# A perceiver block on one core: a key-first head with half loads, and the last tile's sums split between engines

## The reference

```python
q = (layernorm(x) @ Wq + bq)           # per head
k, v = ctx @ Wk + bk, ctx @ Wv + bv
scores = einsum('bqhd,bkhd->hbqk', q, k) / sqrt(32)
attn = softmax(scores.reshape(16 * 4, 128, 2048), axis=0)
x = x + einsum('hbqk,bkhd->bqhd', attn, v) @ Wo + bo
```

## Time and profile before

| | before |
|---|---|
| time, median of 3 runs (lowest to highest) | 725.75 us (724.75 to 725.82) |
| the profiled execution: time, span | 725.73 us, 723.9 us |
| PE busy | 707.0 us (98%) |
| DVE busy | 627.9 us (87%) |
| POOL busy | 502.2 us (69%) |
| ACT busy | 489.7 us (68%) |
| DMA | 55.74 MB, mean 77 GB/s |

### The profile page before, as it was taken

The page is one execution under the profiler, slowest core; times in us unless marked ns, Lnnn a source line. Parts: engine busy times, 40 slices in busy tenths (PEclk is TensorE's granted clock), DMA queues, the critical chain, the costliest instruction groups (busy, mean ns, idle before and its releaser), DMA issues.

```text
span 723.9 us, 17414 instructions
## 1 busy us (share of the span) xinstructions
PE 707.0 (98%) x7587; PEld 570.3 (79%) x7587; DVE 627.9 (87%) x511; ACT 489.7 (68%) x696; POOL 502.2 (69%) x284
## 2 busy tenths in 40 slices
PE   9999999999999999999999999999999999899987
PEld 8777788888888888888888888887677667778876
DVE  6479999999999999999999999999977467977785
ACT  5578677686776867777686776868543446735682
POOL 0165979999999999999999999995993020054400
PEclk9999999999999999999999999999999999999999
DMA  8310110101101010110101101010002799621101
GB/s 333 129 60 8 53 59 2 60 1 60 43 17 60 2 59 1 60 60 1 60 2 59 41 20 60 2 59 2 2 9 110 278 391 382 252 104 59 59 2 59
DMA packets 15387, 55.74 MB, mean 77 GB/s; under 512 B 1616, under 2 KB 2128, under 8 KB 11728
## 3 DMA queue, kind: packets, MB, share of 16 engines
q1 hardware_dynamic: 15312, 54.64, 20.7%
HBM read 43.16 MB, written 11.47 MB: 75 GB/s over the span
## 4 chain that ended last, share of the span: by engine, by line
PE 79%; DVE 7%; DMA 5%; ACT 4%; POOL 3%; issue 1%; SPq 0%; POOLq 0%; DVEq 0%; ACTq 0%
PE ps L464 24%; PE ps L392 23%; PE ps L497 9%; PE ps L523 8%; DMA rel_scratch<-blocks 5%; POOL s_buf L1307 2%; PE ps L437 2%; PE ps L799 2%; PE ps L373 2%; PE ps L533 1%; PE ps L781 1%; PE ps L381 1%; PE ps L547 1%; DVE extra L1482 1%; PE ps L406 1%
## 5 line engine op out<-in xcount | busy, mean ns | idle before, releaser
L1307 POOL TENSOR_TENSOR s_buf<-s_buf,r_all 128x1024 f32<-128x1024 f32 x93 | 197.2, 2158 | 0.8 <-DVE r_all L1495 0.8
L989 ACT COPY s_buf<-ps 128x1024 f32<-128x1024 f32 x128 | 123.1, 1016 | 27.6 <-PE ps L497 27.6
L1005 ACT ACTIVATE s_buf<-s_buf 128x1024 f32<-128x1024 f32 x128 | 134.3, 1064 | 11.1 <-DVE s_buf L1475 8.0
L1453 DVE TENSOR_REDUCE extra<-s_buf 128x128 f32<-128x2048 f32 x48 | 109.3, 2278 | 4.6 <-ACT s_buf L989 4.6
L1475 DVE TENSOR_TENSOR s_buf<-s_buf,ps 128x2048 f32<-128x2048 f32 x48 | 106.9, 2283 | 0.5
L1274 POOL TENSOR_TENSOR v_buf<-v_buf,extra 128x512 f32<-128x512 f32 x64 | 81.0, 1300 | 6.6 <-ACT v_buf L981 6.6
L1482 DVE TENSOR_REDUCE ps<-s_buf 128x128 f32<-128x4096 f32 x16 | 70.8, 4428 | 14.4 <-ACT s_buf L1005 14.4
L981 ACT COPY v_buf<-ps 128x512 f32<-128x512 f32 x64 | 37.6, 587 | 66.2 <-PE ps L392 65.6
L1285 POOL TENSOR_TENSOR w_lo<-raw,w_hi 128x2048 fp32r<-128x2048 f32 x5 | 23.1, 4621 | 83.5 <-ACT w_hi L956 83.5
L497 PEld LDWEIGHTS ps<-q_t,k_t 32*128 32x128 f32 x2048 | 63.0, 186 | 18.9 <-issue 18.9
L497 PE MATMUL ps<-q_t,k_t 32*128 32x128 f32 x2048 | 75.1, 283 | 0.4 <-ACT k_t L971 0.2
(11 more groups left out here) (244 smaller groups left out, 1469.8 us busy)
## 6 DMA issues: line engine op xcount, KB each, us to landing
rel_scratch<-blocks SPq DMA_DIRECT2D x16, 636.0 KB, 10.9
s_buf<-rel_scratch SPq DMA_DIRECT2D x7, 1210.0 KB, 9.7
raw<-in_ctxT SPq DMA_DIRECT2D x8, 1024.0 KB, 4.9
extra<-in_ctxT SPq DMA_DIRECT2D x8, 1024.0 KB, 4.8
raw<-in_Wq SPq DMA_DIRECT2D x2, 1024.0 KB, 6.5
raw<-in_Wv SPq DMA_DIRECT2D x2, 1024.0 KB, 4.8
extra<-in_EvRel SPq DMA_DIRECT2D x1, 2048.0 KB, 13.1
extra<-rel_scratch SPq DMA_DIRECT2D x1, 1210.0 KB, 9.8
```

What stands on the lines that cost most here:

```text
L989: copy(piece(t, 2 * w + u).rearrange("p e (u n) -> p (e u) n", u=2), ps[:, 2 * u:2 * u + 2, :]).then_inc(s["s_evac"], 1)
L1005: nc.scalar.activation(piece(t, p), piece(t, p), ACT.Exp).then_inc(s["exp_done"], 1)
L1307: pool.tensor_tensor(part, part, spread(r_all, 4), ALU.mult).then_inc(s["attn_pool"], 1)
L1453: nc.vector.tensor_reduce(m_ps if k == 0 else m_next[:, k % 2, :], over_pairs(t, 2 * k, 2), AX.XY, ALU.max).then_inc(s["max_done"], 1)
```

## The change

The head. The first halves (columns 0 and 1 of the four input chunks c) of Wk and of the context's first tile are loaded ahead of x, the other halves behind it, and Wq comes after. TensorE starts with the key projection of tile 0 in two halves (`first_keys`), for all four head groups at once in banks 4 to 7, with the transposes between. The query is then projected one head group at a time (`query`), and a head group's scores follow as soon as its query is there; the first value projection is cut in two around the last scores. ScalarE casts by halves and copies a query group (`query_copy`) between score copies; GpSimd casts Wv in place of ScalarE; VectorE's first work is the low parts of the halves, ahead of LayerNorm.

The last tile. TensorE sums pieces 0 to 2 by products with the identity (`head_sums`), in the place of 28 of the 32 warming products; VectorE sums piece 3 alone, and adds TensorE's sum after one reduction from PSUM (`inverse_last`). GpSimd subtracts the last tile's maximum after two of the six pieces of tile T - 2 instead of after all six, and normalises two pieces of the last tile instead of three, behind one weight piece instead of two; VectorE takes the third.

The two semaphores `wkb_ev_in` and `ctxb_b3_in` are used twice, with waits for 32 at the second use.

```diff
-            return 6 if t == 0 and i % 2 else 4
+            return 4 + i if t == 0 else 4
+        def q_bank(hg):
+            return (4, 6, 7, 4)[hg]
...
+            first, rest = slice(0, C // 2), slice(C // 2, C)
+            load(wk_raw[:, first], a["Wk1"][:, first], "wk_in")
+            load(raw[:, first], a["ctxT"][0][:, first], "ctx_in_0")
             for b in range(B):
                 load(x_res[:, b, :], a["x"][b], f"x_in_{b}")
+            load(wk_raw[:, rest], a["Wk1"][:, rest], "wkb_ev_in")
+            load(raw[:, rest], a["ctxT"][0][:, rest], "ctxb_b3_in")
             load(wq_raw, a["Wq1"], "wq_in")
...
+                if (t, b) == (0, 0):
+                    if products.start == 0:
+                        pe.wait_ge(s["qblk_done"], 2)
+                        pe.wait_ge(s["wkv_hi"], 3)
+                    else:
+                        pe.wait_ge(s["wkv_lo"], 3)
...
-                elif w < 2:
+                elif w < 3:
                     pe.wait_ge(s["attn_dve"], t + w + 1)
-                elif w == 2:
-                    pe.wait_ge(s["attn_dve"], t + 3)
-                    pe.wait_ge(s["attn_pool"], POOL_PIECES * t + 1)
                 else:
-                    pe.wait_ge(s["attn_pool"], POOL_PIECES * t + 3)
+                    pe.wait_ge(s["attn_pool"], POOL_PIECES * t + 2)
                 opens = w % 2 == 1 and t + 2 < T
...
+            def head_sums(n):
+                for p in range(n):
+                    pe.wait_ge(s["exp_done"], 8 * (T - 1) + p + 1)
+                    for u in range(2):
+                        last = mm(ps[:, 1, :], ident[:], piece(T - 1, p)[:, 0, u * D:(u + 1) * D], start=p + u == 0,
+                                  stop=p == n - 1 and u == 1, skip_group_check=True)
+                last.then_inc(s["s_psum"], 1)
...
+            def first_keys(k, n):
+                u, v = PARTS[n]
+                if n == 0:
+                    pe.wait_ge(s["wkv_hi"], k + 1)
+                    pe.wait_ge(s["ctx_hi"], 2 * k + 2)
+                elif v:
+                    pe.wait_ge(s["wkv_lo"], k + 1)
+                else:
+                    pe.wait_ge(s["ctx_lo"], 2 * k + 2)
+                for hg in range(C):
+                    for c in (2 * k, 2 * k + 1):
+                        last = mm(ps[:, k_bank(0, hg), :], w_parts[v][:, 0, c, hg * P:(hg + 1) * P], x_parts[u][:, c, :],
+                                  start=(k, n, c) == (0, 0, 0), stop=(k, n, c) == (1, 2, C - 1), skip_group_check=True)
+                    if (k, n) == (1, 2):
+                        last.then_inc(s["kv_psum"], 1)
+            def query(hg, n):
+                u, v = PARTS[n]
+                if n == 0:
+                    if hg == 0:
+                        pe.wait_ge(s["x_hi_done"], C)
+                        pe.wait_ge(s["wq_split"], 2)
+                    if hg < C - 1:
+                        pe.wait_ge(s["kv_evac"], (1, 3, 4)[hg])
+                    else:
+                        pe.wait_ge(s["qblk_done"], 1)
+                elif v:
+                    pe.wait_ge(s["wq_split"], 3)
+                else:
+                    pe.wait_ge(s["xq_split"], B)
+                for c in range(C):
+                    last = mm(ps[:, q_bank(hg), :], (wq_hi, wq_lo)[v][:, c, hg * P:(hg + 1) * P], (xq_hi, xq_lo)[u][:, c, :],
+                              start=n == 0 and c == 0, stop=n == 2 and c == C - 1, skip_group_check=True)
+                if n == 2:
+                    last.then_inc(s["q_psum"], 1)
...
+            keep_warm(3, 14)
+            for n in range(3):
+                first_keys(0, n)
+            transposes(y_ln0, 0, 0)
+            transposes(y_ln0, 0, 1)
+            first_keys(1, 0)
+            transposes(y_ln0, 0, 2)
+            transposes(y_ln0, 0, 3)
+            first_keys(1, 1)
+            first_keys(1, 2)
+            query(0, 0)
             pe.wait_ge(s["tab_mul"], 1)
             pe.wait_ge(s["ones_done"], 1)
+            pe.wait_ge(s["xq_split"], 1)
+            mm(ps[:, 0, 0:2 * P - 1], r_all[0:HD, :], pos_w[0:HD, 0:2 * P - 1], start=True,
                stop=True).then_inc(s["pos_psum"], 1)
+            query(0, 1)
+            query(0, 2)
...
-            project_k(0, 0)
-            for w in range(1, C):
-                project_k(0, w)
-                score(0, w - 1)
-            project_v(0, 0)
+            for w in range(C - 1):
+                query(w + 1, 0)
+                score(0, w)
+                query(w + 1, 1)
+                query(w + 1, 2)
+            project_v(0, 0, slice(0, AHEAD))
             score(0, C - 1)
+            project_v(0, 0, slice(AHEAD, 3 * C))
...
             project_v(T - 1, 3)
+            head_sums(SUMMED)
             attend(T - 2, 2)
             gather(3)
             attend(T - 2, 3)
             residual_in(0)
             residual_in(2)
-            keep_warm(1, 32)
+            pe.wait_ge(s["sum_done"], 3 * T + 1)
+            keep_warm(1, 4)
...
+            first_weight_hi(0, "wk_in")
+            first_ctx_hi(0, "ctx_in_0")
+            ln_std(0, 0)
+            ln_std(0, 1)
+            first_weight_hi(1, "wkb_ev_in")
+            ln_std(0, 2)
+            first_ctx_hi(1, "ctxb_b3_in")
+            ln_std(0, 3)
+            query_hi(0)
+            query_hi(1)
+            act.wait_ge(s["wq_in"], 16)
+            copy(wq_hi[:, 0:2], wq_raw[:, 0:2]).then_inc(s["wq_split"], 1)
+            query_hi(2)
+            query_hi(3)
             act.wait_ge(s["cols_in"], 16)
             act.wait_ge(s["ln_done"], B)
-            act.wait_ge(s["wkv_lo"], 2)
-            k_copy(0, 0)
+            for hg in range(C):
+                k_copy(0, hg)
+            act.wait_ge(s["qadd_done"], 1)
+            query_copy(0)
             ctx_split(1, 0)
+            ctx_split(1, 1)
+            act.wait_ge(s["wkv_lo"], 3)
             for w in range(1, C):
-                k_copy(0, w)
-                ctx_split(1, w)
                 s_copy(0, w - 1)
+                query_copy(w)
+                if w == 1:
+                    ctx_split(1, 2)
+                    ctx_split(1, 3)
+            s_copy(0, C - 1)
...
+            pool.wait_ge(s["wv_in"], 16)
+            pool.wait_ge(s["wkv_hi"], 2)
+            pool.tensor_copy(w_hi[:, 1], wv_raw).then_inc(s["wkv_hi"], 1)
...
-            def normalise(t):
+            def normalise(t, first=8 - POOL_PIECES, end=8):
                 pool.wait_ge(s["r_done"], 2 * t + 1)
-                for p in range(8 - POOL_PIECES if t < T - 1 else 5, 8):
+                for p in range(first, end):
...
-                if t >= 1:
+                if 1 <= t < T - 1:
                     normalise(t - 1)
+                elif t == T - 1:
+                    normalise(t - 1, end=4)
                 if 2 <= t < T - 1:
                     late_add(t - 1, 1)
                 subtract(t)
+                if t == T - 1:
+                    normalise(t - 1, first=4)
...
             out_weight_lo(0)
+            normalise(T - 1, first=6)
             out_weight_lo(1)
-            normalise(T - 1)
             out_weight_lo(2)
...
+            first_weight_lo(0)
+            first_ctx_lo(0)
             moments0(0)
             moments0(1)
...
-            dve.wait_ge(s["wq_split"], 2)
-            tt(wq_lo[:], wq_raw, wq_hi[:], ALU.subtract).then_inc(s["wq_split"], 1)
+            first_weight_lo(1)
+            first_ctx_lo(1)
...
-                p, n = ((0, 4), (4, 2), (6, 2))[k]
+                p, n = (((0, 4) if t < T - 1 else (SUMMED, 4 - SUMMED)), (4, 2), (6, 2))[k]
...
+            def inverse_last():
+                t = T - 1
+                dve.wait_ge(s["sum_done"], 3 * t + 2)
+                tt(r_ps, r_ps, z_next[:, 1, :], ALU.add).then_inc(s["z_steps"], 1)
+                total(t, 2)
+                dve.wait_ge(s["s_psum"], C * T + 1)
+                nc.vector.tensor_reduce(m_next[:, 0, :], ps[:, 1, :].rearrange("p (u q v) -> p q u v", u=2, v=2), AX.XY,
+                                        ALU.add).then_inc(s["sum_done"], 1)
+                dve.wait_ge(s["sum_done"], 3 * t + 3)
+                dve.wait_ge(s["z_steps"], 2 * t + 1)
+                tt(r_ps, r_ps, z_next[:, 0, :], ALU.add).then_inc(s["z_steps"], 1)
+                dve.wait_ge(s["sum_done"], 3 * t + 4)
+                dve.wait_ge(s["z_steps"], 2 * t + 2)
+                tt(r_ps, r_ps, m_next[:, 0, :], ALU.add).then_inc(s["z_steps"], 1)
+                dve.wait_ge(s["z_steps"], 2 * t + 3)
+                dve.wait_ge(s["attn_pool"], POOL_PIECES * t)
+                nc.vector.reciprocal(r_all[:], r_ps).then_inc(s["r_done"], 1)
+                dve.wait_ge(s["r_done"], 2 * t + 1)
+                nc.vector.tensor_copy(r_ps, r_all[:]).then_inc(s["r_done"], 1)
             def normalise(t):
                 dve.wait_ge(s["r_done"], 2 * t + 2)
-                for p, n in ((0, 2),) if t < T - 1 else ((0, 2), (2, 2), (4, 1)):
```

(1 more changed line is left out.)

125 lines of the change are left out of this document (53 added, 72 removed).

## The result

The changed kernel takes **720.34 us** (median of 6 runs, 720.13 to 721.09), the kernel before in the same series 725.4 us (724.66 to 725.89). The ratio is 0.9932, with a 95% interval of 0.992 to 0.9944. The forecast was 722.0, in a range of 720.8 to 724.4: right in sign, 1.66 us too high, and 0.46 us outside the range. The profiled execution took 720.23 us with a span of 718.4; that of the kernel before took 725.73, 0.33 above its median of six. So the two profiles are 5.50 us apart, the medians 5.06.

A forecast was written before the change was run, and what follows sets the result against it. TensorE, busy throughout stage 1's middle, was taken as the bound, so time could come only from the head and last tile: 725.73 - 2.3 (head) - 1.4 (last tile) = 722.0 us, range 720.8 to 724.4.

The forecast's parts named there:

- The head: Start of stage 1: keys fill the gap before 13.1, so tile 1's keys start at 41.5, 2.3 us less.
- rounds: Head: 12 query products plus a score block per head group, kept at 4.05 us each.
- the position product: Head, TensorE: waits 0.8 us for VectorE's table product, ending at 22.4; the one new wait there.
- Passed on through the loop: Stage 1 after the head: everything shifts by TensorE's 2.3 us, and the 0.90 us score-copy wait at 83.99 stays.
- The tail: Last tile: the reciprocal starts at 528.25 instead of 529.65, 1.4 us less (bounds 0.9 and 1.6).
- The PSUM reduction: Last tile, VectorE: new 128x512 reduction from PSUM, taken as 0.7 us.
- the cover of TensorE: Last tile: 1.5 us remain before attention to tile 15, so TensorE's sums cost nothing.
- the way to the reciprocal: Last tile, VectorE: sums, PSUM reduction and two adds lead to the reciprocal at 528.25.
- Rival B: Head loads: half loads are slow, second context half lands 3.4 us later, TensorE stands 2.4; 724.4 us, chance 0.10.
- Rival E: Head: slow clock, each of 48 first key products costs 0.227 us more; 732 us, chance 0.05.
- 725.73 - 2.3 - 1.4: Whole kernel: profiled time before, less the head's and the last tile's gains, gives 722.0 us; chance 0.72.
- the low end: Bottom of the range, 720.8 us: forecast less 0.9 (the 83.99 wait gone) and 0.3 of smaller waits.

The follow-up runs named there:

- before's second: The kernel before, unchanged, profiled once more: 725.3 us.
- whole_loads: The changed kernel with Wk and the context each loaded in one piece ahead of x: 722.71 us, ratio 0.9964.
- head_only: The changed kernel with the last tile as in the kernel before: 722.49 us, ratio 0.9959.
- tail_only: The kernel before with the change's last tile: 722.63 us, ratio 0.9964.
- padded: The changed kernel plus 34 TensorE products of 4 columns, 20 in the head and 14 in the last tile: 728.7 us, ratio 1.0057.
- fewer_warm_tail: The kernel before with 24 instead of 32 warming products in the last tile: 727.38 us, ratio 1.0026.
- sums_no_order: The changed kernel with GpSimd normalising all six pieces of tile 14 before the subtraction, TensorE still summing: 724.77 us, ratio 0.9994.
- the counter-test: Same run as `wide_warm_tail`: the kernel before with fewer, partly wider warming products in the last tile: 724.52 us, ratio 0.9991.
- wide_warm_tail: The kernel before with 8 warming products of 128 columns and 6 of 512 replacing 32 of 128 in the last tile: 724.52 us, ratio 0.9991.
- order_no_sums: The changed kernel with GpSimd's new order, but VectorE summing pieces 0 to 3 and 32 warming products again: 726.14 us, ratio 1.0004.

## Why the prediction missed

**Stage 1 was right**: 3.80 us by the first store of stage 2 in the first pair of profiles, 3.57 over both pairs, forecast 3.7. Its terms were off by little, with opposite signs, so that the sum is closer than its parts.

- *The head, 2.3 forecast.* Measured 1.99 at tile 1's keys in the first pair of profiles, 1.6 against before's second. First keys at 8.08 (8.0), pitch 0.227, rounds 4.04 (4.05). The step that was short is the chain of VectorE's low parts: its second two context pieces took 2.13 us instead of the 1.29 of the first two, so the table product ended at 22.9, not 22.4, and the position product waited 1.02, not 0.8. The first of the two took 1.52 instead of 0.68, while GpSimd's cast of the second half of Wq ran beside it:

```profile
15.58 2.13 DVE L1489 TENSOR_TENSOR x_lo<-raw,x_hi 128x512 fp32r<-128x512 f32 x2
```

```profile
14.89 1.67 POOL L1342 CAST wq_hi<-s_buf 128x1024 fp32r<-128x1024 f32 x1 [13.42 <-DMA s_buf<-in_Wq]
```

In the kernel before this cast came at 9.42, beside no such piece. In `whole_loads` the pair took 2.99 us, there beside GpSimd's cast of Wv (17.06 to 19.34). That the cast is the cause is read from this overlap alone: no run takes it away, and the piece ahead (the low part of the weight, 14.44, 1.22 us) ran beside the same cast without loss. The forecast had named only the cast of Wv. The warming took 4.97 and 6.21 us in the two profiles where 5.9 was forecast, and the wait behind it took that up. That before's own head moves by 0.7 us from run to run (tile 1's keys at 43.04 to 43.74 in its five profiles) I did not know.
- *Passed on through the loop.* Right: 1.99 at tile 1's keys, 2.12 at the wait of 81.87, which stays, and 2.13 at the end (1.99 and the 0.14 of `head_only`).
- *The tail, 1.4 forecast, 1.66 measured* (`tail_only`). The PSUM reduction took 0.68 (0.7), and the cover of TensorE 1.26 (1.5). What was over-priced is the way to the reciprocal: it starts at 525.87, and 528.25 less the head's 2.1 would be 526.1.
- *Rival B* fell, but halves do move slower per byte. The first half of the context landed 1.78 us after that of Wk (ScalarE's casts at 5.01 and 6.79), 0.29 MB/us; whole, 2.42 us (5.69 and 8.11), 0.43 MB/us; and from 3 to 4 us all DMAs together moved 254 GB/s with halves and 426 with whole loads. The Trainium skill ("DMA: Bandwidth & Descriptors", Rules for kernel authors) asks for 1 MiB or more in a DMA, and in that the traces agree; the x loads share the queue in both. What decided here is that half the data was enough to start 1.3 us earlier.
- *Rival E* did not come about in the change, but its mechanism is real: `whole_loads`, `padded`, `fewer_warm_tail` and `sums_no_order` all show 512-column products that take up to twice their 0.227 us, and granted clocks of 0.50 to 0.57 in the stretches given.

**The step that failed** is one that I did not write down as a term: that everything behind stage 1 shifts one for one with it, in "725.73 - 2.3 - 1.4". The sum ended at the attention to tile 15, and the low end, "forecast less 0.9 and 0.3 of smaller waits", held only waits of stage 1. Behind it lay 1.38 + 0.32 us, over both pairs 1.22 + 0.32. Some 0.7 of that is the stalled issue: 0.7 is the difference of the averages to the load of Wk, and the counter-test gives 0.65 in the medians, with an interval that just reaches nothing. The issue of the first load of `rel_scratch` took 1.5 us longer whenever an instruction packet fell 0.3 us ahead of it, and where the packet falls goes with the number of TensorE instructions before, which the change lowered by 76 records. The row was in the trace of the kernel before, 1.93 us for an issue whose neighbours take 0.36 to 0.66; no step of the prediction uses it.

A smaller part of the miss is the level: the sum starts from 725.73, and the median of all six runs of the kernel before is 725.40. Of the 1.66 us, some 0.3 is that, and the rest is the 1.5 us behind stage 1, less the 0.13 by which stage 1 falls short over both pairs (profiles and medians differ by 0.1 in this).

What remains stays open. In stage 2 it is 0.5 to 0.7 us: profiles without the stall differ by 0.95 us there, where the transfers fill the DMA engines (in the change the DMA share is 1.0 from 572 to 586 us). The 0.32 lies behind the issue of the last stores, at the end of the kernel: from there to the end of the span it is 5.1 us in the four profiles with both the old head and the old tail (before twice, `fewer_warm_tail`, `wide_warm_tail`) and 4.8 in the twelve others. So it is neither the stall, which `padded` has and `wide_warm_tail` has not, nor anything that stage 2 passes on.

## What to carry to other kernels

Follow the sum to the end of the kernel: where a later stage is bound by transfers, look for its issues that take much longer than their neighbours, and put their excess into the range: here edits of TensorE's idle-time products alone took it away and brought it. An engine's filler work is part of the design: ask of each piece of it which wait it shortens, since a wait grown from 1.8 to 3.2 or 3.6 us cost 2 us more in clock, and two waits of 2.0 us in `order_no_sums` brought the slow clock as well. And a gain in two parts should be tested crosswise; here the order of GpSimd brought 0.5 us alone and the sums less than nothing, both together 1.66.

## What was not expected of the hardware

- An issue on SyncE's queue took 1.93 to 2.02 us instead of 0.41 in the four profiles where one packet of the instruction queue (0.02 MB) lay 0.3 us ahead of it, and in none of the twelve others. The issues of stores with such a packet as close ahead were not longer.
- TensorE's clock fell while the engine was busy: in `padded` 20 products of 4 columns filled 6.23 us from 6.86 on. In the first part of that stretch the granted clock is 1.00, in the second 0.50, and it stays there over the first keys.

```profile
6.86:9.39 2.53, 2.53 (x26) 2.53 (x24) 2.31 (x5) 1.04 (x2) 0.00 (x0) 1.00 1.05 415
9.39:12.90 3.51, 3.51 (x18) 3.51 (x19) 3.37 (x10) 2.60 (x6) 0.00 (x0) 0.50 1.04 431
12.00:16.00 4.00, 4.00 (x13) 3.41 (x13) 3.89 (x9) 1.52 (x4) 1.27 (x1) 0.50 1.05 397
```

- The time that the first 22 warming products take, and so the moment at which they turn fast, varied from 6.87 to 7.82 us between executions. The change's own two profiles show it in one microsecond, 5 to 6: 12 records of warming products in the first, 7 in the second, the same program. A head in which a wait for data follows them hides this; the old one passed it on in four of its five profiles.

```profile
5.00:6.00 1.00, 1.00 (x12) 1.00 (x11) 0.00 (x0) 0.99 (x1) 0.00 (x0) 1.00 0.96 309
```

```profile
5.00:6.00 1.00, 1.00 (x7) 1.00 (x7) 0.00 (x0) 0.96 (x1) 0.00 (x0) 1.00 0.82 289
```
